# A recommender tower on one core: unblocking and dense layers a quarter later, small banks behind the products, lookups in runs

## The reference

```python
e = jnp.stack([tbl_0[ids[:, 0]], ..., tbl_25[ids[:, 25]]], axis=1)
combined = jnp.concatenate([dense_features[:, None, :], sparse_features], axis=1)
interactions = jnp.einsum('bfd,bgd->bfg', combined, combined)
interactions_flat = interactions[:, _TRIU_I, _TRIU_J]
z = jnp.concatenate([dense_features, interactions_flat], axis=1)
h = jnp.concatenate([z, r_dense_features], axis=1)
h = jnp.maximum(h @ W_top1 + b_top1, 0.0)     # 607 -> 512
h = jnp.maximum(h @ W_top2 + b_top2, 0.0)     # 512 -> 256
y = h @ W_top3                                # 256 -> 1
```

## Time and profile before

| | |
|---|---|
| median, lowest, highest of 3 runs | 520.28, 514.35, 523.56 us |
| the profiled execution's own time | 515.3 us |
| its span, first to last instruction | 513.2 us |
| mean granted TensorE clock | 0.88 of full speed |
| PE busy | 408.8 us (80%) |
| DVE, ACT, POOL busy | 262.7, 208.7, 254.1 us |

### The profile page before, as it was taken

How to read it: one execution, slowest core, us unless ns; L and a number is a source line. 1 busy time by engine, 2 the same in 40 slices (tenths; PEclk the granted TensorE clock), 3 DMA queues, 4 the chain that set the end, 5 groups by cost and what they waited for, 6 DMA issues and landing times.

```text
span 513.2 us, 14192 instructions
## 1 busy us (share of the span) xinstructions
PE 408.8 (80%) x6280; PEld 365.9 (71%) x6280; DVE 262.7 (51%) x323; ACT 208.7 (41%) x436; POOL 254.1 (50%) x265
## 2 busy tenths in 40 slices
PE   5886727777978598875978788887989689789977
PEld 4776716767878497764967687785878588778755
DVE  3789505654555554663553655655364655454220
ACT  3456302234343543444342553435243543337432
POOL 5778875551555555552555535553555535540000
PEclk8998857776999898988897978997898969899989
DMA  6994251230322222221222212221232212210000
GB/s 170 227 240 107 67 158 50 70 108 23 74 59 78 56 64 68 69 64 32 64 66 70 63 49 64 67 74 49 68 68 69 63 42 70 58 39 1 4 1 0
DMA packets 27972, 36.34 MB, mean 71 GB/s; under 512 B 9151, under 2 KB 21959, under 8 KB 27912
## 3 DMA queue, kind: packets, MB, share of 16 engines
q1 hardware_dynamic: 19704, 18.65, 14.6%
q0 software_dynamic: 8192, 16.79, 13.5%
q10 hardware_dynamic: 16, 0.01, 0.0%
HBM read 35.42 MB, written 0.01 MB: 69 GB/s over the span
## 4 chain that ended last, share of the span: by engine, by line
PE 71%; issue 13%; ACT 4%; SPq 4%; DMA 4%; DVE 2%; another core or an unknown queue 1%; ACTq 0%; DVEq 0%
PE ring L411 17%; PE ring L412 15%; PE gram L449 10%; PE ring L485 8%; PE ring L431 7%; PE ring L494 6%; DMA dense<-in_r_dense_features 4%; PE ring L483 3%; SPq L281 2%; PE ring L461 2%; PE ring L472 2%; DVE pairs_and_more L674 2%; PE ring L503 2%; ACT pairs_and_more L578 1%; SPq L275 1%
## 5 line engine op out<-in xcount | busy, mean ns | idle before, releaser
L359 POOL DMA_INDIRECT rows<-in_tbl,ids_all x256 | 248.7, 971 | 201.1 <-PE gram L449 127.3
L651 DVE TENSOR_TENSOR onehot<-idb,vrow 125x1024 fp32r<-125x1024 f32 x160 | 192.7, 1222 | 130.5 <-PE ring L412 58.7
L411 PE MATMUL ring<-onehot,table_hi 125*128 125x256 f32 x608 | 181.6, 328 | 22.1 <-DVE pairs_and_more L674 7.6
L412 PE MATMUL ring<-onehot,table_lo 125*128 125x256 f32 x608 | 169.5, 309 | 0.0
L411 PEld LDWEIGHTS ring<-onehot,table_hi 125*128 125x128 f32 x608 | 132.9, 219 | 28.8 <-issue 8.7
L412 PEld LDWEIGHTS ring<-onehot,table_lo 125*128 125x128 f32 x608 | 133.4, 219 | 0.8
L559 ACT COPY xt<-ring 128x256 f32<-128x256 f32 x80 | 54.2, 677 | 128.9 <-PE ring L412 68.3
L449 PE MATMUL gram<-xt 128*27 128x26 f32 x4096 | 55.1, 201 | 42.6 <-issue 40.0
L449 PEld LDWEIGHTS gram<-xt 128*27 128x27 f32 x4096 | 47.8, 114 | 51.7 <-issue 46.0
L567 ACT COPY xt<-ring 128x512 f32<-128x512 f32 (+1 forms) x56 | 51.2, 987 | 24.1 <-remote 16.0
L431 PE MATMUL ring<-ident,rows 128*128 128x128 f32 x256 | 38.6, 285 | 13.6 <-issue 6.7
(11 more groups left out here) (41 smaller groups left out, 209.7 us busy)
## 6 DMA issues: line engine op xcount, KB each, us to landing
ids_spread<-in_ids_t SPq DMA_DIRECT2D x70, 128.0 KB
rows<-in_tbl,ids_all POOLq DMA_INDIRECT x256
xt<-in_tbl SPq DMA_DIRECT2D x6, 448.0 KB
w<-in_tbl SPq DMA_DIRECT2D x3, 448.0 KB
rows<-in_ids_t SPq DMA_DIRECT2D x10, 128.0 KB, 5.7
dense<-in_r_dense_features SPq DMA_DIRECT2D x16, 64.0 KB
w<-in_W_top SPq DMA_DIRECT2D x4, 256.0 KB
w<-in_W_top SPq DMA_DIRECT2D x1, 512.0 KB
```

Source lines behind the costliest of these rows:

```text
L359: pool.indirect_dma_start(rows[:, i % ROWS, :], None, aps[f"tbl_{f}"], bass.IndirectOffsetOnAxis(ap=ids_all[:, k, f:f + 1].bitcast(U32), a ...
L411: pe.matmul(ps, table_hi[:, m, c * KC + k, :], chosen, start=first, stop=False)
L412: last = pe.matmul(ps, table_lo[:, m, c * KC + k, :], chosen, start=False, stop=final)
L651: dve.tensor_tensor(onehot[:, (CH * u + c) % SLOTS], idb[0:VP, u % 2, 0:BS].unsqueeze(1).to_broadcast([VP, KC, BS]), vrow[:, c * KC:(c + 1 ...
```

## The change

The order in `stages()` is written anew. The unblocking of block n-1 moves from Q3 of its own block to Q0 of block n; its pairs move to Q1, layer 1 to Q1 and Q2, layer 2 to Q2 and Q3, layer 3 stays in Q3. In every quarter the small banks stand first and the lookups in a run at the end: 3, 2, 2 and 3 of them. The first tile's rows of the next block are split over Q2 and Q3. The three pairs banks become two and the four layer-1 banks two. DVE writes one-hot chunks half a lookup further ahead. The copies of products swap engines and become a stage of their own ("grams"): DVE takes steps 0 and 2, ACT 1 and 3; that of step 0 waits until the last unblock bank of the block before is transposed, since A has one place. One rows bank a block moves from DVE to ACT. In block 0 the ids of the ten lookups come by one transfer of 10 rows and are spread by PE with a matmul each into `idb`, in place of ten spreading transfers and ten casts; with them go POOL's waits for those places in `rows`. The dense rows are loaded between the tables, not behind them.

```diff
-        yield from lookups(0, *range(NL - 2))
-        yield from rows(0, 0, 0, 1)
-        yield from lookups(0, NL - 2)
-        yield from rows(0, 0, 2, 3, 4)
+        yield "first_ids", 0, 0, 0
+        yield "first_ids", 0, 1, 0
+        for m in range(NL - 1):
+            yield from lookups(0, m)
+            if m + 2 < NL:
+                yield "first_ids", 0, m + 2, 0
+        yield from rows(0, 0, 0, 1, 2, 3, 4)
         yield from lookups(0, NL - 1)
         for n in range(NB):
             yield "products", n, 0, 0
...
+            if n < NB - 1:
+                yield from layer("unblock", n - 1, 0, 1, 2, 3)
+                yield "grams", n, 0, 0
+                yield from rows(n, 1, 0)
+                yield from lookups(n + 1, 0, 1, 2)
+
+                yield "products", n, 1, 0
+                yield "grams", n, 1, 0
+                yield from layer("pairs", n - 1, 0, 1)
+                yield from rows(n, 1, 1, 2)
+                yield from layer("layer1", n - 1, 0)
+                yield from rows(n, 1, 3, 4)
+                yield from lookups(n + 1, 3, 4)
+
+                yield "products", n, 2, 0
+                yield "grams", n, 2, 0
+                yield from layer("layer1", n - 1, 1)
+                yield from rows(n + 1, 0, 0, 1)
                 yield from layer("layer2", n - 1, 0)
-
-            yield "products", n, 2, 0
-            yield from lookups(n + 1, 5)
-            if n < NB - 1:
+                yield from lookups(n + 1, 5, 6)
+
+                yield "products", n, 3, 0
+                yield "grams", n, 3, 0
+                yield from layer("layer2", n - 1, 1)
+                yield from rows(n + 1, 0, 2, 3, 4)
+                yield from layer("layer3", n - 1, 0)
+                yield from lookups(n + 1, 7, 8, 9)
...
-        return g == 1 or (t, g) == (1, 3)
+        return t == 1 and g in (1, 3)
...
+            sp.dma_start(first_ids_i, aps["ids_t"][:, 0:BS]).then_inc(first_ids_landed, 16)
             sp.dma_start(ids_all[:], ids.rearrange("(t p) f -> p t f", p=P)).then_inc(ids_landed, 16)
             for m in range(NL):
-                spread_ids(m)
                 load_raw(m)
-            load_dense(0)
-            load_dense(1)
+                if m in (3, 6):
+                    load_dense(m // 4)
...
-                    u, first = divmod(i - IDS0, IDS_ROWS)
-                    if 0 <= u < NL and first == 0:
-
-                        pool.wait_ge(idb_ready, u + 1)
...
                 dve.wait_ge(gram_ready, n * STEPS + s + 1)
+                if s == 0 and n > 0:
+
+                    dve.wait_ge(ring_filled, filled("unblock", n - 1, NU - 1, 0))
...
             one_hot(0, 0, 1)
+            one_hot(1, 0)
             for stage, n, a, b in stages():
                 if stage == "lookup":
                     u = n * NL + a + 1
+                    if u < NL and u not in FROM_RAW:
+                        lower_part(u)
+                    elif u >= NL and u - NL in FROM_RAW[:2]:
+                        lower_part(u - NL)
                     if u < NB * NL:
-                        one_hot(u, 0)
-                        if u < NL and u not in FROM_RAW:
-                            lower_part(u)
-                        elif u >= NL and u - NL in FROM_RAW[:2]:
-                            lower_part(u - NL)
                         one_hot(u, 1)
+                    if u + 1 < NB * NL:
+                        one_hot(u + 1, 0)
```

173 lines of the change are left out of this document (86 added, 87 removed).

## The result

| | before | changed |
|---|---|---|
| median of 4 runs | 519.9 us | 532.48 us (531.39 to 537.12) |
| ratio, 95% interval | | 1.032 [1.026, 1.039] |
| profiled execution: own time, span | 515.3, 513.2 us | 532.12, 530.3 us |
| end of block 0's first and second products step | 52.2, 79.8 us | 53.6, 80.5 us |
| rest of block 0 | 46.4 us | 40.0 us |

(Q3's means are over blocks 1 to 5; block 6 has no burst in its Q3, which took 11.4 and 11.9 us.) The spans differ by 17.1 us: start +0.7, the rest of block 0 -6.4, blocks 1 to 6 +21.7, end +1.1. Of the 21.7, Q0 holds 6 x 3.6 = 21.6.

A forecast was written before the change was run, and what follows sets the result against it. Gathers holding products back (about 12.9 us a quarter) and PE's late results were taken as the bound. 515.3 - 7 - 7 - 19.9 + 0.4 + 1 = 482.8 us, plus 2 for the median: 485 us, range 464 to 507.

The forecast's parts named there:

- block-4 reading: From block 4's timelines: gathers hold products back, and PE's results are known 2.7 and 3.5 us late while gathers run.
- The floor: A quarter with a gather burst cannot be shorter than about 12.9 us, whatever PE has to do in it.
- the wait for late results in Q0 and Q3: Blocks 1 to 6: no added wait in these quarters; Q0 12.9 us instead of 13.1, Q3 12.9 instead of 17.4.
- late stretch: From about 5 us until 11.5 us after a burst's start, other engines see PE's results late.
- The start: Start and block 0's Q0: -7 us, at most 7.6 and at least nothing, as POOL finishes its 48 gathers sooner.
- block 0's Q3: Block 0's last quarter: 13 us instead of 20.3, a gain of 7 us.
- Q1 and Q2 in the mean: Blocks 1 to 5: Q1 15.0 us instead of 13.9, Q2 13.8 instead of 12.9.
- the end: Behind block 6: +1 us, as block 7 also gets block 6's unblocking and pairs.
- The edits put at nothing: Fuller banks, the rows bank moved to ScalarE and the products copy's new wait: no change in time.
- The signs: Wrong if quarters fall below 12.9 us, Q3 stays above 15 or Q0 is longest; block 0's second step ending at 71 to 74.
- Rival (b): Late stretch hits every run of lookups: each quarter with a burst takes 15.2 us, 526 us in all; chance 0.07.
- The clock: By the skill's loop-order rule alone, runs of lookups would give back all time at 1.2 GHz; the floor mostly hides it.

The follow-up runs named there:

- e13: Changed kernel with its four unblock banks back in Q3 of their own block; 551.18 us in the slow condition, 1.066 of the kernel before.
- e17: Changed kernel with four chunk slots and a new order, two unblock banks in Q0 and two in Q1; 511.2 us, slow condition, 0.955 of the kernel before.
- e3: Changed kernel with four one-hot chunk slots instead of three and 37 places for rows instead of 45; 515.19 us, slow condition, 0.965 of the kernel before.
- e1: Changed kernel gathering only tiles 0 to 2 (48 gathers instead of 256); 434.93 us in the slow condition, 0.815 of the kernel before.
- e5: Changed kernel without any edit, timed in the fast condition; 414.86 us against 405.39 us for the kernel before, ratio 1.024.
- e14: Changed kernel with only Q0 reordered, its three lookups directly behind the products; 540.07 us in the slow condition, 1.047 of the kernel before.
- e16: Kernel before the change with four chunk slots and 37 places for rows; 515.36 us in the slow condition, ratio 1.001.

## Why the prediction was wrong

- **The block-4 reading was right in its kind.** Products reached inside a burst end about 12.9 us after it starts, and results of PE are seen late in it. The floor showed in Q0 of e13 and e17 and in Q1 and Q2 of e3, and block 0's second step was held in the same way. What I took for a property of the gathers is one of the gathers in the slow condition: it needs both (e1, e5).
- **The step that failed is the wait for late results in Q0 and Q3, which the prediction put at nothing.** It had found that results are late from about 5 to 11.5 us after a burst's start and priced that in Q1 and Q2, but for Q0 it had "In the first 5 us I take the delay as none" and "the last but one known free at 7 us: PE is done at 9.3". Lookup 0 ended 4.4 us after the burst's start and was seen at 8.6, so the late stretch sets in a little sooner than the prediction took it. The next result, which the last chunk needs, came 5.3 us after the start, inside the prediction's own late stretch, and was seen at 11.5; the prediction had PE done at 9.3. Q0 took 16.6 us for 12.9, 22.0 us in six blocks. For Q3 the prediction let three chunks follow one another at DVE's pace, with no late result at all, though its lookups 7 and 8 ended 5.7 and 7.6 us after the burst's start; it took 17.3 for 12.9, 22.1 us in five. These two are 44 of the 49.6 us between the forecast change of the span, -32.5, and the measured +17.1. Two smaller terms are in them: the half clock behind the wait (1.3 us in block 4's Q0) and 0.75 us for the store of lookup 9 in Q3, both left out of the sum.
- **The start: -7 forecast, +0.7 came.** Lookup 6, for which POOL waits, ended at 40.01 and not some us sooner than 35.87, and the second products step again ended only behind the 48 gathers. The lower end of the bound (nothing) was right. That the lookups beside the first gathers wait for late results too (lookup 3's store came 4.6 us late) was not priced; in e5, where nothing is late, lookup 6 ended at 34.10.
- **Right:** block 0's Q3 (14.1 for 13, from 20.3), Q1 and Q2 in the mean (14.5 for 15.0, 13.7 for 13.8, though single blocks took 12.8 to 15.8) and the end (+1.1 for +1). The edits put at nothing were not tried by themselves.
- **The signs.** Q3 stayed above 15 us, which the prediction itself named as a sign of being wrong, and block 0's second step ended at 80.5, not at 71 to 74.
- **Rival (b), at 0.07, comes nearest:** the runs of lookups lie in the stretch in which results come late. It gave 526 us, deciding from a mean quarter of 14.7 us on; the 23 quarters with a burst took 15.5 on average. Its 15.2 for every quarter fits none of the four: Q1 and Q2 stayed below it and Q0 and Q3 went above. The mechanism was written down and then set aside, on the ground that three chunks are ready in Q0 and Q3 and the first slots free before 5 us. That covers half of a run of six.
- **A cost of the order itself was in no case.** Without late results the changed order is 2.4% slower as well. The prediction put PE's order at no cost under the floor, and where there is no floor it has one: the store of the last lookup, which rows and pairs used to cover (0.76 us a block, as much as the 4.5 us of added idle time in six blocks), and 6.0 us in six blocks of longer busy time, whose cause stays open. In the slow condition the store's 0.75 us stands in every Q3 too. Whether the longer busy time costs anything there is not shown; it may be hidden under the floor.
- **The clock.** PE's granted clock over blocks 1 to 6 is 0.89, where the lines of the earlier trace rows average 0.90. Q3 of block 4 rose from 0.78 to 0.91, and Q0 fell from 0.96 to 0.80, behind PE's wait. The Trainium skill, TensorE: Matmul & The Clock Gate, section "Loop structure matters more than you think", says that the order of the loops decides whether matmuls stay warm, and that long waits between them let the clock fall. Q0 agrees, as PE's idle time there grew from 1.5 to 4.7 us. That runs of lookups give back all time at 1.2 GHz, as the prediction worked out from it, did not come out: these runs wait.

What stays open: what brings about the slow condition and by what path a result of PE is held up in it.

## What to carry to other kernels

When an answer to one engine is late in a certain stretch, don't count what work fits there; list each thing that waits for an answer (a slot, a bank, an activation), and when the work that it waits for ends. Moving work ahead of such a chain pushes the chain into the stretch (e13), and reordering the chain moves the wait to its next member (e14). Splitting the moved work shortened it here (e17); another buffer did in the changed order (e3) and not in the one before (e16). And run both kernels on more than one occasion: here the same two programs differ by 3.2% in one condition and 2.4% in another for partly different reasons.
